# Loads of x issued from GpSimd instead of SyncE, and a ScalarE copy of the FFN split in two

## The chip, the cores and the metric

The kernel runs on the 8 cores of one Trainium2 chip. The cores run the same program on different data and exchange nothing. The metric is the device time of one execution, in microseconds (us), of the slowest core.

## The reference, cut to what matters

```python
# x: (4, 4096, 2048); D = 2048, 16 heads of 128, FFN width 8192
def attn(x):
    q, v = x @ Wq, x @ Wv                      # per head of 128 columns
    state[0] = v[0]; state[s] = lam * state[s-1] + v[s]      # lam = sigmoid(beta), per head
    y = layernorm(q * state) * ln_g + ln_b
    return (y * silu(x @ Wg)) @ Wo
def ffn(x):
    h = silu(x @ w_gate) * (x @ w_up)
    h = keep_the_2_largest_of_each_4(h)        # by absolute value
    return h @ w_down
x = x + layernorm(attn(layernorm(x)))
x = x + layernorm(ffn(layernorm(x)))
```

## The kernel before, in words

Each core has one half of one batch row: 2048 positions, as 16 tiles of 128. A core with a second half needs the state at its start, which it computes from the first half (`xprev`; zeros for the other cores). All weights come as float32 from HBM and are cast to bfloat16 in SBUF. Two SBUF slots, `wslotA` and `wslotB`, hold one 2048x2048 weight each. The stages, one after another:

- **Setup and weights.** `load_square_weight` brings Wq into `wslotA` and Wv into `wslotB`, each in 32 halves of 512 KB (`load_half`, line 606). SyncE issues the load into one of four staging quarters; ScalarE (line 617) and VectorE (line 613) take turns to cast. `lnab_bcast` (line 362) then brings ln_g and ln_b and spreads each over the partitions with matmuls (line 368) and a cast.
- **Carry prologue** (line 382): for each tile of `xprev`, load, layernorm, cast, and a matmul with decay weights that GpSimd (`iota`, line 394) and ScalarE make; then 256 small matmuls with Wv give `carry`.
- **Scan stage** (`attn_qv_scan`, line 443): for each tile `prep` loads x (line 446), takes statistics (line 310) and normalizes into `fp2`; TensorE transposes (line 336), ScalarE copies to SBUF (line 341), TensorE projects with Wq into PSUM `psB` and with Wv into `psA` (line 356), a matmul per head does the scan. ScalarE's copy of it (line 476) goes to VectorE, which multiplies by q (line 478), layernorms, and applies ln_g and ln_b (lines 496 and 499); GpSimd stores the result in `s_yaff` (line 502).
- **Gate stage** (`attn_gate`, line 505): Wg is loaded into `wslotA`. In iteration t TensorE transposes x(t) and projects it; `drain_ygT(t-1)` transposes the gated tile t-1 out of its `fp` buffer (line 336, VectorE evacuates at line 346) and GpSimd stores it in `s_ygT` (line 511); `prep(t+1)` loads x(t+1) into that same `fp` buffer (line 516) and normalizes it (line 519); ScalarE takes the silu (line 536), GpSimd loads `s_yaff` (line 538), VectorE multiplies (line 540).
- **Output stage** (`attn_out`, line 546): the first FFN weights (`load_q`) and Wo are loaded. In iteration t SyncE loads `s_ygT` (line 573) into `bp[t % 2]`, TensorE projects (line 356), `drain_xn3T(t-1)` transposes `fp2` (line 557), ScalarE copies it into `bp[(t-1) % 2]` (line 562) and GpSimd stores it in `s_xn3T` (line 566). VectorE layernorms the projection, x is loaded (line 586) and added (line 589), the sum goes to `s_x2` (line 592, shown as `s_x` in the trace) and is layernormed again (line 595). The load of ygT(t+1) takes the buffer that the store of xn3T(t-1) reads.
- **FFN** (`ffn`, line 638): 8 chunks of 1024 of the 8192 columns. For each chunk and tile: load `s_xn3T` (line 718), 32 gate matmuls (line 727), silu (line 732), 32 up matmuls (line 740), product (line 750), absolute value (line 755), nine VectorE instructions for the 2:4 mask (lines 765 to 788). Two tiles later (one in the last chunk) comes `drain`: 8 transposes of h into `psA` (line 675), a ScalarE copy back into h's own buffer as bfloat16 (line 680), 32 down matmuls into `psB` (line 689), VectorE's evacuation (line 697), and a store from GpSimd that adds into `s_acc` (lines 700 and 704). In the last chunk the final layernorm and addition follow.

**What sets the order.** `Prog.op` records operations; each engine runs its own in the order in which they are written, and a DMA belongs to the engine that issues it. An operation waits, by semaphores, for the last writer of each resource (`Res`) that it reads, and for the last writer and all readers since of each that it writes. The engine's own earlier instructions are waited for too, on all engines but TensorE. A resource has only one last writer:

```python
        for r in reads:
            if r.w is not None:
                toks.append(r.w)
...
        for w in writes:
            w.w = tok
            w.r = []
```

While an instruction waits, all that stands behind it on its engine waits, DMA issues included. SyncE issues all weight loads, the x loads, the `s_ygT`, `s_xn3T`, `s_acc` and `s_x2` loads and the output; GpSimd issues the stores to scratch tensors, the `s_yaff` loads and a few iotas.

## Time and profile before

| | |
|---|---|
| median of 2 runs | 6746.96 us (6743.37 to 6750.54) |
| the profiled execution | 6750.88 us |
| its span, slowest core (core 0) | 6749.3 us |
| spans of the 8 cores | 6694.7 to 6749.3 us |
| mean granted TensorE clock, core 0 | 0.856 |
| TensorE matmul busy | 4224.4 us (63%) |
| VectorE busy | 2060.5 us (31%) |
| ScalarE busy | 1003.0 us (15%) |
| GpSimd busy | 162.6 us (2%) |

The span runs from the first to the last instruction of a core. Busy shares are means over stages with different limits. All cores have nearly the same span, so core 0 stands for them. In the rows below the engines are PE (TensorE matmul), PEld (its weight loads), DVE (VectorE), ACT (ScalarE), POOL (GpSimd), and SPq for SyncE's issues of DMAs; L356 is line 356.

### The profile page before, as it was taken

The numbers are of one execution on the slowest core, as the hardware profiler recorded it, in microseconds if no ns is written. First come the engines' busy times: TensorE is split into PE (matmuls) and PEld (weight loads), VectorE is DVE, ScalarE is ACT, GpSimd is POOL, SyncE is SP. The second block draws the span as 40 slices with busy tenths as digits, with TensorE's granted clock in tenths as the row PEclk, the third lists the DMA queues.
The fourth block names the chain that finished last, engine by engine and source line by source line (L and its number), as shares of the span: only waits on it lengthen the run. The fifth ranks groups of instructions, "written<-read, shape, count | busy, mean of one in ns | idle before, by whom it ended". The sixth has DMA issues, their size and how long they took to land.

```text
span 6749.3 us, 51690 instructions; the slowest of 8 cores (6694.7 to 6749.3 us)
## 1 busy us (share of the span) xinstructions
PE 4224.4 (63%) x19374; PEld 1999.6 (30%) x19374; DVE 2060.5 (31%) x2796; ACT 1003.0 (15%) x1033; POOL 162.6 (2%) x232
## 2 busy tenths in 40 slices
PE   0236888456616668678678588498488487444443
PEld 0013444234303334334334234244244243111111
DVE  1533333212214433333333233233233233222222
ACT  2301111111111011111111111211211111111010
POOL 0000000000000000000000000000000000000000
PEclk9999888778758889889889799799799799777776
DMA  5300010222353331433533623623523534422223
GB/s 159 136 17 25 35 38 32 72 90 77 106 189 115 126 109 66 146 97 66 151 92 66 173 70 73 180 57 75 174 60 84 159 66 114 139 82 77 79 74 103
DMA packets 140830, 649.31 MB, mean 96 GB/s; under 512 B 15652, under 2 KB 15652, under 8 KB 107812
## 3 DMA queue, kind: packets, MB, share of 16 engines
q1 hardware_dynamic: 110630, 461.44, 20.9%
q0 software_dynamic: 29952, 184.56, 12.4%
q8 instruction: 156, 2.56, 0.2%
q14 instruction: 92, 0.75, 0.0%
HBM read 453.00 MB, written 192.94 MB: 96 GB/s over the span
## 4 chain that ended last, share of the span: by engine, by line
PE 59%; DMA 20%; DVE 10%; ACT 5%; issue 4%; SPq 1%; DVEq 0%; ACTq 0%; POOL 0%; POOLq 0%
PE psB L689 15%; PE psA L727 14%; PE psA L740 12%; PE psB L356 9%; PE psA L356 5%; DMA stg<-w_up 4%; DMA stg<-w_down 2%; PE psA L336 2%; DMA bp<-s_xn3T 2%; DMA s_acc<-wslotB 2%; ACT bp L755 2%; DMA stg<-Wo 1%; DVE stats L310 1%; DMA fp<-x 1%; DMA stg<-Wg 1%
## 5 line engine op out<-in xcount | busy, mean ns | idle before, releaser
L727 PE MATMUL psA<-wslotA,bp 128*128 128x512 bf16 x4096 | 954.4, 393 | 701.5 <-DMA bp<-s_xn3T 701.5
L740 PE MATMUL psA<-wslotA,bp 128*128 128x512 bf16 x4096 | 904.9, 379 | 0.0
L727 PEld LDWEIGHTS psA<-wslotA,bp 128*128 128x128 bf16 x4096 | 410.7, 101 | 1227.7 <-issue 778.0
L740 PEld LDWEIGHTS psA<-wslotA,bp 128*128 128x128 bf16 x4096 | 400.9, 98 | 483.2
L689 PE MATMUL psB<-wslotB,l_mat 128*128 128x512 bf16 x1440 | 344.6, 401 | 278.6 <-DVE bp L768 243.1
L356 PE MATMUL psB<-wslotA,bp 128*128 128x512 bf16 x2048 | 489.6, 404 | 44.2 <-ACT bp L341 44.2
L689 PE MATMUL psB<-wslotB,t_mat 128*128 128x512 bf16 x1472 | 357.9, 406 | 215.1 <-DVE bp L768 195.8
L356 PE MATMUL psA<-wslotB,bp 128*128 128x512 bf16 x1536 | 355.1, 394 | 212.5 <-DMA bp<-s_ygT 212.5
L697 DVE COPY wslotB<-psB 128x2048 f32<-128x2048 f32 x128 | 293.3, 2291 | 451.3 <-PE psB L689 451.3
L689 PE MATMUL psB<-wslotB,fp 128*128 128x512 bf16 x1184 | 280.4, 398 | 187.1 <-DVE bp L768 170.4
L732 ACT ACTIVATE fp<-psA 128x1024 f32<-128x1024 f32 x128 | 131.1, 1024 | 1510.8 <-PE psA L727 1510.7
L336 PE MATMUL psA<-ident,fp 128*128 128x128 f32 x768 | 145.0, 369 | 264.0 <-DVE fp L519 213.2
L356 PEld LDWEIGHTS psB<-wslotA,bp 128*128 128x128 bf16 x2048 | 208.2, 103 | 320.6 <-issue 111.4
L689 PEld LDWEIGHTS psB<-wslotB,l_mat 128*128 128x128 bf16 x1440 | 144.3, 102 | 467.5 <-issue 323.3
L613 DVE CAST wslotA<-stg 128x1024 bf16<-128x1024 f32 x160 | 111.0, 694 | 550.7 <-DMA stg<-w_up 322.8
L356 PEld LDWEIGHTS psA<-wslotB,bp 128*128 128x128 bf16 x1536 | 154.4, 101 | 408.7 <-issue 240.6
L689 PEld LDWEIGHTS psB<-wslotB,t_mat 128*128 128x128 bf16 x1472 | 148.8, 103 | 412.5 <-issue 268.6
L617 ACT CAST wslotA<-stg 128x1024 bf16<-128x1024 f32 x160 | 166.9, 1044 | 444.3 <-DMA stg<-w_gate 292.3
L750 DVE TENSOR_TENSOR t_mat<-psA,fp 128x1024 f32<-128x1024 f32 x46 | 56.3, 1224 | 568.0 <-PE psA L740 568.0
L310 DVE BATCH_NORM_STATS2 stats<-fp 128x6 f32<-128x512 f32 x256 | 158.0, 681 | 230.2 <-DMA fp<-s_acc 222.2
L750 DVE TENSOR_TENSOR l_mat<-psA,fp 128x1024 f32<-128x1024 f32 x45 | 55.1, 1225 | 545.3 <-PE psA L740 545.3
L689 PEld LDWEIGHTS psB<-wslotB,fp 128*128 128x128 bf16 x1184 | 117.7, 101 | 340.4 <-issue 220.4
(128 smaller groups left out, 3198.5 us busy)
## 6 DMA issues: line engine op xcount, KB each, us to landing
s_acc<-wslotB POOLq DMA_DIRECT2D x128, 1024.0 KB, 7.8
stg<-w_gate SPq DMA_DIRECT2D x128, 512.0 KB, 5.4
stg<-w_up SPq DMA_DIRECT2D x128, 512.0 KB, 5.9
stg<-w_down SPq DMA_DIRECT2D x128, 512.0 KB, 6.2
bp<-s_xn3T SPq DMA_DIRECT2D x128, 512.0 KB, 3.3
fp<-x SPq DMA_DIRECT2D x48, 1024.0 KB, 5.3
stg<-Wq SPq DMA_DIRECT2D x32, 512.0 KB, 4.6
stg<-Wv SPq DMA_DIRECT2D x32, 512.0 KB, 4.5
```

What stands on the lines that cost most here:

```text
L310: ins = v.bn_stats(st6[:, 6 * i:6 * i + 6], src_ap[:, 512 * i:512 * (i + 1)])
L336: ins = t.transpose(psA[:, half * 1024 + j * 128:half * 1024 + (j + 1) * 128], src_ap[:, kc * 128:(kc + 1) * 128], ident[:])
L356: ins = t.matmul(psum[:, n * 512:(n + 1) * 512], xT_ap[:, kc, :], w_sb[:, kc, n * 512:(n + 1) * 512], start=(kc == 0), stop=(kc == KC - 1))
L613: P.op("vector", lambda v, dst_ap=dst_ap, k=k: v.tensor_copy(dst_ap, wstg4[k]), reads=[r_wstg4[k]], writes=[dst_res, r_wstg4[k]])
L617: P.op("scalar", lambda s, dst_ap=dst_ap, k=k: s.copy(dst_ap, wstg4[k]), reads=[r_wstg4[k]], writes=[dst_res, r_wstg4[k]])
L689: ins = tt.matmul(psB[:, n * 512:(n + 1) * 512], hT[:, kc, :], fdc[:, kc, n * 512:(n + 1) * 512], start=(kc == 0), stop=(kc == ICW // 128 ...
L697: P.op("vector", lambda v, ev=ev: v.tensor_copy(ev[:], psB[:]), reads=[r_B[0], r_B[1]], writes=[r_stgF[dk], r_B[0], r_B[1]])
L727: ins = tt.matmul(psA[:, n * 512:(n + 1) * 512], xT[:, kc, :], fgc[:, kc, n * 512:(n + 1) * 512], start=(kc == 0), stop=(kc == KC - 1))
L732: P.op("scalar", lambda s, fx=fx: s.activation(fpool[fx][:, 0:ICW], psA[:, 0:ICW], AF.Silu), reads=[r_A[0]], writes=[r_fp[fx], r_A[0]])
L740: ins = tt.matmul(psA[:, 1024 + n * 512:1024 + (n + 1) * 512], xT[:, kc, :], fuc[:, kc, n * 512:(n + 1) * 512], start=(kc == 0), stop=(kc ...
L750: P.op("vector", lambda v, fx=fx, hsl=hsl: v.tensor_tensor(hsl[:, 0:ICW], psA[:, ICW:2 * ICW], fpool[fx][:, 0:ICW], ALU.mult), reads=[r_A[ ...
L755: P.op("scalar", lambda s, hsl=hsl: s.activation(habs[:, 0:ICW], hsl[:, 0:ICW], AF.Abs), reads=[rht], writes=[r_bp[2]])
```

## The change

First, six places at which SyncE issued a DMA now have GpSimd issue it: ln_g, ln_b, the tiles of `xprev`, and the tiles of x in the scan, the gate and the output stage. That is 2 + 16 + 48 loads. What they wait for and where they go stays. Second, in `drain`, the copy of 1024 columns is written as two copies of 512, each of which also writes a resource of its own, `rc[0]` or `rc[1]`, and the four groups of down matmuls read `rc[0]`, `rc[0]`, `rc[1]`, `rc[1]` besides `rh`.

```diff
     def lnab_bcast():
-        P.op("sync", lambda s: s.dma_start(out=fpool[0][0:1, :], in_=lng_d[:, :]), dma=True,
+        P.op("gpsimd", lambda g: g.dma_start(out=fpool[0][0:1, :], in_=lng_d[:, :]), dma=True,
              writes=[r_fp[0]])
...
-        P.op("sync", lambda s: s.dma_start(out=fpool[0][0:1, :], in_=lnb_d[:, :]), dma=True,
+        P.op("gpsimd", lambda g: g.dma_start(out=fpool[0][0:1, :], in_=lnb_d[:, :]), dma=True,
              reads=[r_fp[0]], writes=[r_fp[0]])
...
     def carry_prologue():
...
-            P.op("sync", lambda s, t=t, fx=fx: s.dma_start(
+            P.op("gpsimd", lambda g, t=t, fx=fx: g.dma_start(
                 out=fpool[fx][:], in_=xprev_d[t * 128:(t + 1) * 128, :]),
...
     def attn_qv_scan():
...
-            P.op("sync", lambda s, t=t, fx=fx: s.dma_start(
+            P.op("gpsimd", lambda g, t=t, fx=fx: g.dma_start(
                 out=fpool[fx][:], in_=x_d[t * 128:(t + 1) * 128, :]), dma=True,
                 writes=[r_fp[fx]])
...
```

The same edit stands in `prep` of `attn_gate` and, before the add, in `attn_out`. Then, in `drain`:

```diff
-            P.op("scalar", lambda s, hT_flat=hT_flat: s.copy(hT_flat[:, 0:ICW],
-                                                             psA[:, 0:ICW]),
-                 reads=[r_A[0]], writes=[rh, r_A[0]])
+            rc = [Res(), Res()]
+            for hh in range(2):
+                P.op("scalar", lambda s, hT_flat=hT_flat, hh=hh: s.copy(
+                    hT_flat[:, hh * 512:(hh + 1) * 512],
+                    psA[:, hh * 512:(hh + 1) * 512]),
+                     reads=[r_A[0]], writes=[rh, rc[hh], r_A[0]])
...
-                P.op("tensor", f, reads=[rh, r_fdc[q]], writes=[r_B[0], r_B[1]])
+                P.op("tensor", f, reads=[rh, rc[q // 2], r_fdc[q]],
+                     writes=[r_B[0], r_B[1]])
```

GpSimd's order in the gate stage, before (`bp3` holds the transposed gated tile, `bp2` the tile of `s_yaff`):

```order
L538 DMA bp2<-s_yaff 128x2048 [waits d_gpsimd5,d_gpsimd6]
L511 DMA s_ygT<-bp3 128x2048 [waits c_vector,d_gpsimd7]
L538 DMA bp2<-s_yaff 128x2048 [waits d_gpsimd8]
L511 DMA s_ygT<-bp3 128x2048 [waits c_vector,d_gpsimd9]
L538 DMA bp2<-s_yaff 128x2048 [waits d_gpsimd0]
```

And now (`fp0` and `fp1` are the buffers of x):

```order
L516 DMA fp0<-x 128x2048 [waits d_gpsimd5,d_gpsimd0]
L516 DMA fp1<-x 128x2048 [waits d_gpsimd7]
L538 DMA bp2<-s_yaff 128x2048 [waits d_gpsimd9,d_gpsimd2]
L511 DMA s_ygT<-bp3 128x2048 [waits c_vector]
L516 DMA fp0<-x 128x2048 [waits c_tensor,d_gpsimd4]
L538 DMA bp2<-s_yaff 128x2048
```

From the third load on, each load of x stands between a store of ygT, which waits for VectorE, and a load of yaff. The x loads had been alone on SyncE in this stage.

GpSimd's order in the output stage, before (`s_x2` is the stored sum, `s_xn3T` the transposed second layernorm):

```order
L566 DMA s_xn3T<-bp0 128x2048 [waits c_scalar,d_gpsimd9]
L592 DMA s_x2<-fp1 128x2048 [waits c_vector,d_gpsimd0]
L566 DMA s_xn3T<-bp1 128x2048 [waits c_scalar,d_gpsimd1]
L592 DMA s_x2<-fp0 128x2048 [waits c_vector,d_gpsimd2]
L566 DMA s_xn3T<-bp0 128x2048 [waits c_scalar,d_gpsimd3]
```

And now:

```order
L566 DMA s_xn3T<-bp0 128x2048 [waits c_scalar,d_gpsimd0]
L586 DMA fp1<-x 128x2048 [waits c_tensor,d_gpsimd1]
L592 DMA s_x2<-fp1 128x2048 [waits c_vector,d_gpsimd2]
L566 DMA s_xn3T<-bp1 128x2048 [waits c_scalar,d_gpsimd3]
L586 DMA fp0<-x 128x2048 [waits d_gpsimd4]
L592 DMA s_x2<-fp0 128x2048 [waits c_vector,d_gpsimd5]
```

The load of x(t) now follows the store of xn3T(t-1), and stands ahead of the store of x2(t).

ScalarE's order in the FFN, before (`t_mat`, `l3_mat` and `fp2` hold h in turn):

```order
L680 CAST t_mat<-psA 128x1024 [waits c_tensor]
L732 ACTIVATE fp1<-psA 128x1024 [waits c_tensor]
L755 ACTIVATE bp2<-t_mat 128x1024 [waits c_scalar,c_vector]
L680 CAST l3_mat<-psA 128x1024 [waits c_tensor]
L732 ACTIVATE fp0<-psA 128x1024 [waits c_tensor]
```

And now, where lines 682, 736 and 759 are what 680, 732 and 755 were:

```order
L682 CAST t_mat<-psA 128x512 [waits c_tensor]
L682 CAST t_mat<-psA 128x512 [waits c_scalar]
L736 ACTIVATE fp1<-psA 128x1024 [waits c_tensor]
L759 ACTIVATE bp2<-t_mat 128x1024 [waits c_vector]
L682 CAST l3_mat<-psA 128x512 [waits c_tensor]
L682 CAST l3_mat<-psA 128x512 [waits c_scalar]
```

The second copy of each pair waits for the first, ScalarE's own.

## Rows read from the trace of the kernel before

**Rows 1.** The page, part 4: the chain by line.
```profile
PE psB L689 15%; PE psA L727 14%; PE psA L740 12%; PE psB L356 9%; PE psA L356 5%; DMA stg<-w_up 4%; DMA stg<-w_down 2%; PE psA L336 2%; DMA bp<-s_xn3T 2%; DMA s_acc<-wslotB 2%; ACT bp L755 2%; DMA stg<-Wo 1%; DVE stats L310 1%; DMA fp<-x 1%; DMA stg<-Wg 1%
```

**Rows 2.** Timeline, gate stage, one tile: start us, us, engine, line [idle before].
```profile
1547.81 2.55 DVE L346 CAST bp<-psA 128x1024 bf16<-128x1024 f32 x2 [16.16 <-PE psA L336]
1548.56 27.73 SPq L516 DMA_DIRECT2D fp<-x  x2
1550.89 0.53 POOL L511 DMA_DIRECT2D s_ygT<-bp  x1 [26.16 <-DVE bp L346]
...
1553.84 1.35 DVE L519 TENSOR_SCALAR fp<-fp,ln1m,ln1r 128x2048 f32<-128x2048 f32 x1 [3.48 <-DMA fp<-x]
...
1560.05 13.97 PE L356 MATMUL psB<-wslotA,bp 128*128 128x512 bf16 x64 [1.25 <-ACT bp L341]
```

**Rows 3.** Timeline, output stage, one tile.
```profile
2112.53 0.53 POOL L566 DMA_DIRECT2D s_xn3T<-bp  x1 [21.16 <-ACT sd L315]
...
2115.41 2.29 DVE L589 TENSOR_TENSOR fp<-fp 128x2048 f32<-128x2048 f32 x1 [0.17 <-DVE fp L581]
2115.58 0.33 SPq L573 DMA_DIRECT2D bp<-s_ygT  x1
...
2119.03 15.27 PE L356 MATMUL psB<-wslotB,bp 128*128 128x512 bf16 x64 [8.54 <-DMA bp<-s_ygT]
```

**Rows 4.** Timelines of ACT and PE, FFN, one steady tile.
```profile
2647.91 0.99 ACT L680 CAST t_mat<-psA 128x1024 bf16<-128x1024 f32 x1
...
2649.15 7.07 PE L689 MATMUL psB<-wslotB,t_mat 128*128 128x512 bf16 x32 [2.76 <-DVE bp L768]
```

**Rows 5.** DMA issues, whole span: KB each, median us from issue to landing.
```profile
fp<-xprev SPq DMA_DIRECT2D x16, 1024.0 KB, 4.9
...
s_yaff<-bp POOLq DMA_DIRECT2D x16, 512.0 KB, 2.9
bp<-s_yaff POOLq DMA_DIRECT2D x16, 512.0 KB, 5.6
```

**Rows 6.** The chain in order of time, projections of the gate stage: start us, us.
```profile
1448.91 15.82 PE psB L356 x64
1478.18 13.97 PE psB L356 x64
...
1778.55 13.97 PE psB L356 x64
```

**Rows 7.** Timeline of DVE, end of the Wv load and start of lnab_bcast.
```profile
206.22 0.69 DVE L613 CAST wslotB<-stg 128x1024 bf16<-128x1024 f32 x1 [4.23 <-DMA stg<-Wv]
213.01 2.29 DVE L373 CAST stg<-psA 128x2048 bf16<-128x2048 f32 x1 [6.10 <-PE psA L368]
```

**Rows 8.** Timeline, carry prologue: GpSimd's second iota, VectorE's statistics of the third tile.
```profile
238.35 0.94 POOL L394 IOTA wlamT<- 16x128 f32 x1 [235.06 <-PE psB L401]
...
246.53 2.47 DVE L310 BATCH_NORM_STATS2 stats<-fp 128x6 f32<-128x512 f32 x4
```

**Rows 9.** Groups by line, scan stage: VectorE's product: busy us, mean ns | idle before us.
```profile
L478 DVE TENSOR_TENSOR stg<-psB,vst 128x2048 f32<-128x2048 f32 x16 | 36.7, 2292 | 443.3 <-ACT vst L476 443.3
```

**Rows 10.** Timeline, start of the gate stage.
```profile
1390.61 1.34 DVE L519 TENSOR_SCALAR fp<-fp,ln1m,ln1r 128x2048 f32<-128x2048 f32 x1 [1.80 <-DMA fp<-x]
```

**Rows 11.** ScalarE's copies out of PSUM: groups by line, and a timeline row.
```profile
L562 ACT CAST bp<-psB 128x1024 bf16<-128x1024 f32 x16 | 16.2, 1012 | 117.4 <-PE psB L557 116.4
...
L423 ACT CAST xbarT<-psB 128x256 bf16<-128x256 f32 x1 | 0.4, 372 | 2.1 <-PE psB L419 2.1
...
2055.65 2.17 ACT L562 CAST bp<-psB 128x1024 bf16<-128x1024 f32 x2 [15.70 <-PE psB L557]
```

**Rows 12.** The chain in order of time, second chunk: first and last slow drain.
```profile
2977.58 8.75 PE psB L689 x32
...
3254.04 8.75 PE psB L689 x32
```

**Rows 13.** Timeline of POOL, end of the gate stage.
```profile
1841.73 0.99 POOL L511 DMA_DIRECT2D s_ygT<-bp  x1 [13.41 <-DVE wslotA L613]
```

More of the change, by code:

```diff
@@ L515, in prep @@
             fx = t % 2
-            P.op("sync", lambda s, t=t, fx=fx: s.dma_start(
+            P.op("gpsimd", lambda g, t=t, fx=fx: g.dma_start(
                 out=fpool[fx][:], in_=x_d[t * 128:(t + 1) * 128, :]), dma=True,
@@ L585, in attn_out @@
                  writes=[r_fp[2], rpso[0], rpso[1]])
-            P.op("sync", lambda s, t=t, fx=fx: s.dma_start(
+            P.op("gpsimd", lambda g, t=t, fx=fx: g.dma_start(
                 out=fpool[fx][:], in_=x_d[t * 128:(t + 1) * 128, :]), dma=True,
```

## The prediction

> **What bounds the kernel now.** I read the page's chain first [rows 1]: most of it is TensorE, spread over all stages, so what an edit is worth must be read inside its stage. Then I took one tile of each stage in the timeline and asked what the first matmul after each gap waited for.
>
> *Gate stage* [rows 2]: after the projection TensorE transposes tile t-1, which frees the buffer, SyncE issues the load of x(t+1) at 1548.56, VectorE normalizes it at 1553.84 as soon as it lands, and after two transposes and copies the next projection starts at 1560.05. The load of x is on the chain. VectorE's two evacuations end at 1547.81 + 2.55 = 1550.36, GpSimd issues the store of ygT at 1550.89 and the load of yaff right behind it, at 1550.89 + 0.53 = 1551.42; those two delay nobody.
>
> *Output stage* [rows 3]: projection t+1 waits for ygT(t+1), loaded by SyncE at 2115.58 as soon as the store of xn3T(t-1), issued by GpSimd at 2112.53, has landed. The x(t) needed by the add at 2115.41 had long been there.
>
> *FFN, steady* [rows 4]: TensorE works without a gap but for one, 2.76 us a tile, between the transposes of h and the down matmuls. ScalarE's copy (2647.91 + 0.99 = 2648.90) ends 0.25 us before the matmuls start (2649.15). The profile names DVE L768 as releaser, an instruction that happens to end nearby; by the code's own waits it is the copy.
>
> **The change part by part.**
>
> **1. x loads on GpSimd, gate stage.** GpSimd issues in program order: store ygT(t-1), load x(t+1), load yaff(t). So x(t+1) now waits for VectorE's evacuations. It takes yaff's slot, which is 1551.42 - 1548.56 = 2.86 us later, and stands behind 512 KB of ygT. 1 MB alone lands in 4.9 us (xprev), 512 KB alone in 2.9 as a store (s_yaff) and in 3.45 as a load (2119.03 - 2115.58) [rows 3, 5], so a further 512 KB costs 1.5 to 2.0; I take 1.8. The pair, 1.5 MB, lands at 1550.89 + 4.9 + 1.8 = 1557.6 instead of 1553.84: +3.8 us. If both move side by side for free, 1551.42 + 4.9 = 1556.3 and +2.5 us; if x is also slowed as bp<-s_yaff is, 5.6 against 2.9, by 2.7, it is more than the pair needs, and I cap it at +4.5. The load is delayed in tiles 2 to 15 (x(0), x(1) are issued before the first store): 14 x 3.8 = +53 us (35 to 63). The last of them no longer competes with w_gate loads: -1.
>
> **2. The clock in that stage.** A projection takes 15.82 us when it starts at the low level (1.2 GHz) and 13.97 when it runs at 2.4 GHz [rows 6]; the 12 from 1478.18 to 1778.55 are all fast. The gap ahead of them grows by more than half. I let half of the 12 start low: 6 x 1.9 = +11 us (0 to 22).
>
> **3. Output stage.** Order on GpSimd: store xn3T(t-1), load x(t), store x2(t). x(t) is now issued at 2112.53 + 0.53 = 2113.06 and moves its 1 MB while xn3T lands and while ygT(t+1), on SyncE's queue, is loaded. Before, the next x stood behind ygT on the same queue and cost it little (3.45 us). If the two queues share, ygT loses the time in which x has the other half: x, alone, is over at about 2113.06 + 4.9 = 2118.0, ygT moves data in the last 1.5 to 2 us of its 3.45, so about 1.2 us are lost; the most contended 512 KB load shows 5.6 against 3.5, 2.1 us [rows 3, 5]. 14 x 1.2 = +17 (0 to 30). The add gets x(t) some 3 to 4 us late (lands 2118 to 2119.5 against 2115.41), with no one waiting: the transposes of that tile come only after the next projection, at 2119.03 + 15.27 = 2134.3 and later. After the last tile nothing covers it: +4 (2 to 6) before the FFN starts. The first ygT no longer shares with two x loads: -1.
> The Trainium skill ("DMA: Bandwidth & Descriptors", section "SWDGE vs HWDGE vs iDMA") says that software and hardware descriptors sit in different internal queues of a DMA engine, which serves them in turn. By that rule ygT shares with x, as I take it; were it first come first served, ygT would wait for all of x's rest and the term would be nearer its upper end. No row of before shows this pair.
>
> **4. Start.** ln_g is needed only by its matmuls, and its load was queued behind the last Wv load. On GpSimd it comes at the very start, the matmuls run during the weight load, and VectorE's cast follows its last weight cast at 206.22 + 0.69 = 206.91 instead of 213.01 [rows 7]: -6 us (the ln_b half keeps its length).
>
> **5. Carry prologue and scan stage.** xprev(t+2) now also waits for GpSimd's iota, over at 238.35 + 0.94 = 239.29, and lands by 239.29 + 0.53 + 4.9 = 244.7; it is used at 246.53 [rows 8]. Nothing, 1.8 us of cover; if 2 us were added per load, a few us in all. In the scan stage x(t+2) waits for the store of yaff(t); VectorE's statistics come some 7 us later, but it idles 443.3 / 16 = 27.7 us a tile after them [rows 9]: nothing.
>
> **6. Entry of the gate stage.** x(0) is no longer behind the Wg loads: -3 (-5 to 0), the 1.80 us that VectorE waited for it [rows 10] and a little bandwidth.
>
> **7. The split copy.** The second half's copy writes rh too, so rh's last writer is the second copy, and the very first down matmul reads rh: it waits for both. rc only matters if rh did not stand beside it. So nothing starts early. The price: 256 columns take 0.372 us, 1024 take 0.99, so 512 take about 0.372 + 256 x (0.99 - 0.372) / 768 = 0.58. The second copy waits for the first one's semaphore; two such copies of the output stage take 2.17 in a row where 2 x 1.012 are work, a gap of 0.15 [rows 4, 11]. 0.58 + 0.15 + 0.58 = 1.31 against 0.99: +0.32 us a drain (0.25 to 0.40). On the path are the 13 steady drains of 7 chunks and 16 of the last, 107 x 0.32 = 34; at the chunk borders are 21 more, where other waits may cover between none and all of 0.32; I take 0.1, +2. Together +36 (27 to 50).
>
> **8. The clock in the FFN.** Of the 13 steady drains of a chunk, 5 run at the low level part of the time, 8.75 us instead of 7.07 (2977.58 the first, 3254.04 the last) [rows 4, 12]. The clock had fallen in the gap; it grows from 2.76 to 3.08. I take 6.5 of 13: 1.5 x 7 x 1.68 = +18 (0, to 8 x 7 x 1.68 = 94 if all do).
>
> **Sum**: 53 - 1 + 11 + 17 + 4 - 1 - 6 - 3 + 36 + 18 = **+128 us** on the profiled 6750.9, which is 3.9 above the median shown, 6747. From the median: **6875 us**, 1.9% slower.
>
> **The rivals.**
> A, *the queues hardly hinder each other*: x costs only its later issue (14 x 2.5 = 35), ygT loses 5, the clock nothing. 35 - 1 + 5 + 3 - 1 - 6 - 3 + 34 = +66, 6813 us. For it: ygT's load hardly suffered from the x load behind it. Against it: yaff's load takes 5.6 us in company.
> B, *the clock decides*: every steady drain falls to the low level. 94 instead of 18: +204, 6951 us. For it: the gap is already one at which 5 in 13 fall. Against: most 2.76 us gaps leave it up, and 0.3 us is little. It passes 2% from about one more slow drain per chunk than I take.
> C, *the split works*: the first matmuls start on the first half, 0.99 - 0.58 = 0.41 us earlier. 107 x 0.41 = -44, the shorter gap spares all slow drains, 35 x 1.68 = -59, and the loads still cost 53 - 1 + 11 + 17 + 4 - 1 - 6 - 3 = +74: -29, 6718 us, not slower. Against: the shared rh.
> D, *GpSimd's issue is stretched by VectorE*: one store issue beside VectorE's casts took 0.99 us instead of 0.53 [rows 2, 13]. 28 x 0.46 = 13 more: 6888 us. Against: in the gate stage VectorE is idle when x is issued. The Trainium skill ("SBUF — State Buffer", the "DVE blocks DMA" box) has this as a rule; by this row the trace agrees in kind.
>
> **How the numbers follow.** Mine 0.60 (0.34 of it within 2%, 0.26 above), A 0.17, B 0.13, D 0.06, C 0.04 (half of it faster by over 2%). 2%, 135 us, about what a measurement of this kernel can tell from no change, ends at 6882. So faster 0.02, same 0.53, slower 0.45. Range 6810 to 6935: it holds A and D and leaves out B and C.
>
> **What would show it.** In the gate stage: x issued by POOL after ygT's store, the tile at 31 us instead of (1778.55 - 1478.18) / 11 = 27.3, and the chain's share of fp<-x larger. Projections of 15.8 among them show part 2. Output stage: the ygT load above 3.5 us. FFN: two copies of about 0.58 us, the gap at 3.1, and the count of 8.7 us drains. I am wrong if the gap falls below 2.76 (C), if the gate tile grows by under 2.5 us, or if the steady FFN tile grows by over 1 us (B).

## The result, and the profile after

The changed kernel is slower: the ratio of its time to that of the kernel before is **1.0295, 95% interval 1.024 to 1.0349**. That is 6946 us on 6747; I had said 6875, with 6935 as the upper end. The direction was right and the size too small. The ratio is taken over six executions of either kernel: 6743 to 6755 us before; five of 6926 to 6940 us and one of 7019 us now. The five alone would give 6929 us, just inside my range, so that the range was missed is less certain than that the sum was too small. The profiled execution took 6936.59 us, with a span of 6934.9 us on core 4, the slowest; the kernel before had 6750.88 and 6749.3 us on core 0. In some executions one half of the chip ran at a lower clock than the other; such executions are left out, but for the one of 7019 us, where the difference was small, and where the experiments name cores 4 to 7, only that half was undisturbed.

The page of the changed kernel: the chain by line, and two rows of the DMA issues (KB each, median us from issue to landing).

```profile
PE psB L692 14%; PE psA L731 13%; PE psA L744 12%; PE psB L356 9%; PE psA L356 5%; DMA stg<-w_up 5%; DMA stg<-w_down 2%; DMA bp<-s_xn3T 2%; PE psA L336 2%; DMA s_acc<-wslotB 2%; DMA fp<-x 1%; DMA stg<-Wg 1%; DMA bp<-s_ygT 1%; DVE stats L310 1%; DMA stg<-Wv 1%
...
bp<-s_xn3T SPq DMA_DIRECT2D x128, 512.0 KB, 3.3
fp<-x POOLq DMA_DIRECT2D x48, 1024.0 KB, 6.8
```

Beside [rows 1] the chain has nearly the same members. bp<-s_ygT and stg<-Wv are new in the list, at 1% each, ScalarE's line 755 (2%) and stg<-Wo (1%) have dropped out of it, and the shares of three lines moved by a point. A change of 2.95% spread over four stages does not stand out in it. So the span is cut at TensorE's own landmarks, start times in the timeline: the first and last projection of a stage, the first gate matmuls of a chunk. The columns before and after are from the slowest core of each trace, and so is the difference; the column beside it takes the means over all 8 cores of the same two traces.

| stretch of the span, us | before | after | difference | 8 cores | predicted |
|---|---|---|---|---|---|
| start to end of the scan's last projection | 1273.4 | 1267.4 | -6.0 | -6.5 | -6 |
| entry: to the start of the first gate projection | 123.6 | 131.7 | +8.1 | +3.3 | -3 |
| gate stage: first to last projection, start to start | 410.0 | 494.0 | +84.0 | +89.6 | +63 |
| from the end of the last to the first output projection | 170.2 | 165.0 | -5.2 | +0.9 | -1 |
| output stage: first to last projection, start to start | 393.1 | 425.9 | +32.8 | +28.9 | +17 |
| from the end of the last to the first gate matmul of the FFN | 48.2 | 51.3 | +3.1 | +4.3 | +4 |
| FFN, 7 chunks | 3376.5 | 3436.7 | +60.2 | +55.3 | +54 with the last |
| FFN, last chunk, to its last down matmul | 893.3 | 902.0 | +8.7 | +11.0 | |
| **sum** | | | **+185.7** | **+186.8** | **+128** |

The sum is the difference of the spans, 6934.9 - 6749.3 = 185.6. (The last projections of the two stages and the tail behind the last down matmul are in no line; they take 61 us in both.) The FFN came nearest (69 against 54); the gate and output stages and the entry are too small by 21, 16 and 11. One pair of cores carries a few us of chance a line: by the means over 8 cores they are too small by 27, 12 and 6.

**Gate stage.** The timeline of one tile.

```profile
1605.29 1.91 PE L336 MATMUL psA<-ident,fp 128*128 128x128 f32 x16
...
1606.57 2.55 DVE L346 CAST bp<-psA 128x1024 bf16<-128x1024 f32 x2 [19.85 <-PE psA L336]
...
1609.73 0.54 POOL L511 DMA_DIRECT2D s_ygT<-bp  x1 [32.30 <-DVE bp L346]
1610.30 0.53 POOL L516 DMA_DIRECT2D fp<-x  x1
1610.82 0.53 POOL L538 DMA_DIRECT2D bp<-s_yaff  x1
1617.39 1.35 DVE L519 TENSOR_SCALAR fp<-fp,ln1m,ln1r 128x2048 f32<-128x2048 f32 x1 [8.27 <-DMA fp<-x]
```

The order is the one forecast: VectorE's evacuations, the store of ygT, x, yaff. From VectorE's start at the evacuations, 1606.57, to the normalization, 1617.39, it is 10.82 us; in [rows 2] it was 1553.84 - 1547.81 = 6.03. That is +4.8 in this tile, where I took 3.8: the issue of x moved as forecast (3.73 us after VectorE's start; before 0.75, so 2.98 later), but the load then needs 1617.39 - 1610.30 = 7.1 us instead of 5.3. As a mean over tiles 2 to 15 it is +4.5 (core 0 before, core 4 now) to +4.7 (core 5 in both), at my cap of 4.5 or just above it. From 1487.53 to 1859.78, eleven tiles, a tile takes 33.8 us, against 27.3 before. The rest is in the projections. TensorE's timeline, three in a row:

```profile
1695.64 12.16 PE L356 MATMUL psB<-wslotA,bp 128*128 128x512 bf16 x54 [0.22 <-issue]
1724.94 13.97 PE L356 MATMUL psB<-wslotA,bp 128*128 128x512 bf16 x62 [1.25 <-ACT bp L341]
1757.37 15.62 PE L356 MATMUL psB<-wslotA,bp 128*128 128x512 bf16 x63 [1.25 <-ACT bp L341]
```

(The first is the second part of a projection that began at 1691.85 and took 15.95 in all; the row is split where a record is missing.) Of the twelve that took 13.97 us in [rows 6], one still does; the others take 15.5 to 16.0. The sum over the third to the fifteenth projection rose from 183.5 to 202.1 us, +18.6. 14 x 4.5 to 4.8 and 18.6 make 82 to 86, of the 84 in the table.

**Entry.** The timeline ahead of the gate stage:

```profile
1285.95 33.34 SPq L610 DMA_DIRECT2D stg<-Wg  x9
1287.31 1.06 POOL L516 DMA_DIRECT2D fp<-x  x2 [0.35 <-issue]
...
1303.19 0.69 DVE L613 CAST wslotA<-stg 128x1024 bf16<-128x1024 f32 x1 [17.32 <-DMA stg<-Wg]
```

The two first x loads are now issued 1.4 us after the first Wg load, and move 2 MB ahead of the Wg loads that follow. SyncE's nine Wg issues, each paced by a staging buffer that comes free, are spread over 33.3 us; in the trace of before the same nine took 23.9. VectorE waits 17.32 us for the first of its halves, against 9.28. I had counted only that x came earlier. The cost is smaller than this pair of cores shows: the entry's mean over 8 cores is 126.1 us before, 129.3 here and 129.7 to 129.8 in the three experiments in which GpSimd loads this x at once (b, c and e below).

**Output stage.** The timeline of one tile:

```profile
2199.54 0.53 POOL L566 DMA_DIRECT2D s_xn3T<-bp  x1 [17.74 <-ACT sd L315]
2200.07 0.53 POOL L586 DMA_DIRECT2D fp<-x  x1
...
2203.08 30.14 SPq L573 DMA_DIRECT2D bp<-s_ygT  x2
...
2207.86 2.29 DVE L589 TENSOR_TENSOR fp<-fp 128x2048 f32<-128x2048 f32 x1 [5.61 <-DMA fp<-x]
2209.56 16.31 PE L356 MATMUL psB<-wslotB,bp 128*128 128x512 bf16 x62 [12.05 <-DMA bp<-s_ygT]
```

ygT is issued at 2203.08 and lets the projection go at 2209.56: 6.48 us, against 3.45 in [rows 3] (as means of the stage's tiles 6.2 and 3.6). The store of xn3T takes 2203.08 - 2199.54 = 3.54 until the buffer is free (3.05 before). TensorE's idle time ahead of a projection rose from 8.65 to 11.55 us, as means over the stage's 15 gaps, +2.9 x 15 = 43. The 16 projections gave 259.5 - 251.7 = 7.8 back, as more of their work fell into fast clock: 43 - 8 = 35, of the 33 in the table. VectorE waits 5.61 us for x(t) and nobody waits for VectorE there, as forecast.

How ygT loses its time is not as forecast. The DMA queues' packets between 2203.4 and 2206.3 us, which begins just after ygT's issue (queue, packets, MB, share of the 16 DMA engines):

```profile
q0 software_dynamic: 99, 0.81, 76.6%
```

and between 2206.3 and 2209.6:

```profile
q1 hardware_dynamic: 144, 0.52, 38.8%
q0 software_dynamic: 34, 0.15, 10.9%
```

q0 is GpSimd's queue and carries x, q1 is SyncE's and carries ygT. For some 3 us ygT does not move at all, while x has the engines; all of ygT's packets come when x is nearly over. Over the stage, ygT's first packet comes 0.96 us after its issue before the change, and 2.7 to 4.1 us after it now. So ygT does not share the engines with x: it waits behind the whole of it.

**FFN.** TensorE's timeline, three steady drains in a row:

```profile
3131.24 7.07 PE L692 MATMUL psB<-wslotB,fp 128*128 128x512 bf16 x32 [3.01 <-ACT fp L682]
3156.00 8.75 PE L692 MATMUL psB<-wslotB,t_mat 128*128 128x512 bf16 x31 [3.01 <-ACT t_mat L682]
3182.45 7.07 PE L692 MATMUL psB<-wslotB,l_mat 128*128 128x512 bf16 x31 [3.01 <-ACT l_mat L682]
```

and ScalarE's:

```profile
3154.50 1.24 ACT L682 CAST t_mat<-psA 128x512 bf16<-128x512 f32 x2
```

The two copies take 1.24 us together (0.99 was one, [rows 4]); the gap is 3.01 us, 0.25 more than the 2.76 before, and this time the profile names the copy itself as the releaser. Nothing starts early. Here drains at 8.75 and at 7.07 us alternate. Counting the down matmuls of the 7 chunks that take over 7.6 us, there are 54 of 112, and were 40. From the first to the last steady drain of each chunk TensorE took 2287.9 us before and 2333 after, +45, which is 91 x 0.25 = 23 and 14 more slow drains x 1.68 = 24 (46 in all).

### The profile page after: what moved, and what is told of

Read it like the earlier page. It is cut to its first block, busy times and chain, and to the rows that moved or that the text cites. A ratio compares the mean times of both kernels' runs of the same rounds, so it can differ in the third digit from the quotient of the medians.

```text
span 6934.9 us, 51439 instructions; the slowest of 8 cores (6895.5 to 6934.9 us)
## 1 busy us (share of the span) xinstructions
PE 4227.8 (61%) x19010; PEld 2008.5 (29%) x19374; DVE 2060.0 (30%) x2796; ACT 1023.0 (15%) x1161; POOL 198.3 (3%) x298
## 4 chain that ended last, share of the span: by engine, by line
PE 58%; DMA 21%; DVE 9%; issue 6%; ACT 5%; SPq 1%; DVEq 0%; ACTq 0%; POOL 0%; POOLq 0%
PE psB L692 14%; PE psA L731 13%; PE psA L744 12%; PE psB L356 9%; PE psA L356 5%; DMA stg<-w_up 5%; DMA stg<-w_down 2%; DMA bp<-s_xn3T 2%; PE psA L336 2%; DMA s_acc<-wslotB 2%; DMA fp<-x 1%; DMA stg<-Wg 1%; DMA bp<-s_ygT 1%; DVE stats L310 1%; DMA stg<-Wv 1%
## 5 line engine op out<-in xcount | busy, mean ns | idle before, releaser
L701 DVE COPY wslotB<-psB 128x2048 f32<-128x2048 f32 x128 | 293.3, 2291 | 507.6 <-PE psB L692 507.6
L336 PEld LDWEIGHTS psA<-ident,fp 128*128 128x128 f32 x768 | 133.6, 198 | 348.1 <-issue 345.0
```

Source lines behind the costliest of these rows:

```text
L336: ins = t.transpose(psA[:, half * 1024 + j * 128:half * 1024 + (j + 1) * 128], src_ap[:, kc * 128:(kc + 1) * 128], ident[:])
L701: P.op("vector", lambda v, ev=ev: v.tensor_copy(ev[:], psB[:]), reads=[r_B[0], r_B[1]], writes=[r_stgF[dk], r_B[0], r_B[1]])
```

## The experiments

What I held after the result: (1) the split copy costs 50 to 70 us and the moved loads the rest, and the two hardly meet; (2) in the gate stage it is the order on GpSimd's queue that delays x, plus the clock; (3) in the output stage it is that x moves at the moment at which ygT does, not who issues it; (4) the number of slow drains follows the gap. Each has its rival in the texts below. Most of the experiments rest on one execution each, so they are read by stage, over its cores, and the difference of the spans is the weaker sign.

### The two halves of the change

`a_split_only` is the kernel before with only the change in `drain`; `b_moves_only` is the changed kernel with that part put back.

```diff
+            rc = [Res(), Res()]
+            for hh in range(2):
+                P.op("scalar", lambda s, hT_flat=hT_flat, hh=hh: s.copy(
...
+                     reads=[r_A[0]], writes=[rh, rc[hh], r_A[0]])
```

> The kernel before with the split copy alone. Theory 1 (the split costs its own gap, and the longer gap makes TensorE's clock fall more often): gap before the down matmuls 3.0 us instead of 2.76, about one steady drain in two at 8.7 us instead of 5 in 13, the FFN 60 to 70 us longer, ratio 1.009 to 1.011. Rival (the FFN grew in the changed kernel because the moved loads shifted it against the clock or the DMAs): only the gap's 0.25 x 128 = 32 us, ratio about 1.005, drains slow as often as before.

Measured: span 6791.8 us, executions of 6793 and 6797 us, beside 6740 and 6750 of the kernel before on the same chip, +43 to +57; but two more of the kernel before took 6779 and 6809 us there, so the times alone would not settle it. The stages ahead of the FFN are as before (gate 408.6, output 390.6 us on core 5). The steady part of the FFN is 2329 to 2336 us over the cores, as in the changed kernel (2331 to 2338), and the slow drains are 51 to 56, one in two, as Theory 1 had it. The whole FFN is 41 us longer by the means over 8 cores, less than the 60 to 70 of Theory 1 and more than the rival's 32.

> The changed kernel with the copy in one piece again: only the loads are moved. Theory 1 (the two edits add up): everything up to the FFN as in the changed kernel, the FFN as before, 6749 + 116 = about 6865 us span, ratio 1.016 to 1.018. Rival (the parts interact, the moved loads also lengthen the FFN): above 1.020.

Measured: span 6858.7 us, executions of 6860 and 6862; ratio 1.0135, interval 1.0039 to 1.0232, slower than the kernel before but too wide to say whether by 2%. Gate 491 to 497 us, output 413 to 422, the FFN's 7 chunks 3361 to 3371 with 40 to 42 slow drains. So the FFN does not feel the moved loads alone, and the stages before it do not feel the split. By the spans the halves give 42.5 + 109.4 = 152 of 186. The rest is in the FFN: by the means over 8 cores it grew by 41 us with the split, by -4 with the moved loads, and by 66 with both. Its steady part is the same in a and in the changed kernel, so these 29 us arise at the chunk borders and in the last chunk, where the halves do meet; how, no run here shows.

### The moved loads, stage by stage

`c_gate_only` and `d_out_only` move the x load of one stage alone. The edit of c, in `attn_gate`; that of d is the same in `attn_out`:

```diff
         def prep(t):
             fx = t % 2
-            P.op("sync", lambda s, t=t, fx=fx: s.dma_start(
+            P.op("gpsimd", lambda g, t=t, fx=fx: g.dma_start(
```

> The kernel before with only the gate stage's loads of x on GpSimd. Theory 1 (the loss lies in that stage's own queue): first to last projection of the stage 494 us instead of 410, its start 8 us later than the end of the scan stage was before, the output stage as before; span about 6749 + 84 + 8 - 5 = 6836. Rival (the stage suffers from what the other moved loads leave behind, a shifted clock or semaphores reused in another order): under +40 in that stage.

Measured: span 6838.7 us, +89. The gate stage takes 493 to 504 us, the entry 128 to 133; the output stage 391 to 400 and the FFN's 7 chunks 3362 to 3377 us. The gate load alone makes that stage's loss. The entry, too: it had been 124 to 129 on the cores of the kernel before, and is 3.7 us longer in the mean.

> The kernel before with only the output stage's loads of x on GpSimd. Theory 1 (x shares the DMA engines with the load of ygT, which the projection waits for): first to last projection of that stage 426 us instead of 393, ygT landing in 6.5 us instead of 3.45, span about 6749 + 33 + 3 = 6785. Rival (the stage is longer only because the gate stage before it changed): 393 us, no change in the time.

Measured: span 6762.7 us, +13, less than expected: the output stage takes 410 to 418 us, 21 more than before in the mean over 8 cores where the changed kernel has 29 more, and the FFN, which this edit does not touch, came out 13 us shorter on the slowest core. The timeline on core 5:

```profile
2113.68 0.53 POOL L566 DMA_DIRECT2D s_xn3T<-bp  x1 [17.43 <-ACT sd L315]
...
2117.07 29.83 SPq L573 DMA_DIRECT2D bp<-s_ygT  x2
...
2123.12 16.61 PE L356 MATMUL psB<-wslotB,bp 128*128 128x512 bf16 x64 [11.47 <-DMA bp<-s_ygT]
```

The load of ygT takes 2123.12 - 2117.07 = 6.05 us, and TensorE waits 11.47: the pattern of the changed kernel, from this one edit.

### Issuer, queue position, or company?

`g_out_x_early` leaves x(t) on GpSimd but records it at the top of the iteration, ahead of `drain_xn3T`, so it is issued at the start of the projection, well before ygT's load.

```diff
+            P.op("gpsimd", lambda g, t=t, fx=fx: g.dma_start(
+                out=fpool[fx][:], in_=x_d[t * 128:(t + 1) * 128, :]), dma=True,
+                writes=[r_fp[fx]])
             if pend is not None:
                 drain_xn3T(pend)
```

> The output stage's loads of x on GpSimd, but recorded ahead of the store of xn3T(t-1), so that they run early, during the projection; all else as before. Theory 1 (ygT lands late because x moves at the same moment): ygT lands in about 3.5 us again, first to last projection 388 to 396 us, span as before. Rival (GpSimd's queue is slower, or more traffic there delays the stores of xn3T): 410 us or more.

Measured, cores 4 to 7: output stage 387 to 393 us, as before the change; spans 6719.8 to 6738.0. Core 5:

```profile
2107.93 27.30 SPq L573 DMA_DIRECT2D bp<-s_ygT  x2
...
2111.34 16.78 PE L356 MATMUL psB<-wslotB,bp 128*128 128x512 bf16 x64 [8.88 <-DMA bp<-s_ygT]
```

3.41 us for ygT, the 3.45 of [rows 3]. GpSimd as issuer costs the path nothing; x just ahead of ygT costs some 2 to 3 us a tile. The Trainium skill ("DMA: Bandwidth & Descriptors", section "SWDGE vs HWDGE vs iDMA") has the engines serve software and hardware queues in turn. If so, a turn here is a whole transfer: no packet of ygT moves between 2203.4 and 2206.3 us, and the load that alone needs 3.45 us takes 6.48 and 6.05 because it waits for x. The section "Issuing engines are not separate DMA queues" of the same page of the Trainium skill says that transfers run on the same engines and interleave whoever starts them. That they meet on the same engines, g and d bear out; that they interleave, the rows of the changed kernel do not show, as there ygT follows x.

`e_gate_x_first` has x on GpSimd ahead of the store of ygT; `f_gate_sync_late` leaves it on SyncE but makes it wait for the evacuations. The edit of e:

```diff
+
+        def store_ygT(t):
             P.op("gpsimd", lambda g, t=t: g.dma_start(out=s_ygT[t], in_=bpool[3][:]),
                  dma=True, reads=[r_bp[3]], writes=[r_sygT[t]])
...
-            P.op("sync", lambda s, t=t, fx=fx: s.dma_start(
+            P.op("gpsimd", lambda g, t=t, fx=fx: g.dma_start(
...
             if t + 1 < NT:
                 prep(t + 1)
+            if pend is not None:
+                store_ygT(pend)
```

and of f:

```diff
                 out=fpool[fx][:], in_=x_d[t * 128:(t + 1) * 128, :]), dma=True,
-                writes=[r_fp[fx]])
+                reads=[r_bp[3]], writes=[r_fp[fx]])
```

> The gate stage's loads of x on GpSimd as in the changed kernel, but each recorded ahead of the store of ygT, so that it waits for TensorE's transposes alone. All other loads as before. Theory 1 (the place in the queue costs, not the engine): x is issued about 2 us after the transposes begin and lands some 5.3 us later, the tile is back at 27.3 to 28 us, first to last projection 405 to 415 us, projections mostly 13.97 us. Rival (a load issued by GpSimd is itself slower): landing near 7 us, tiles of 30 us or more, 450 us.

> The kernel before, all loads on SyncE, but the gate stage's load of x also waits for VectorE's second evacuation, as it does behind the store of ygT. Theory 1 (the wait costs what it lasts, about 2.3 us a tile, the common queue the rest, and the longer gap makes the projections start at the low clock): x issued 2.4 us later, landing in 5.3 to 6 us, tile about 30 us plus 1.7 where the projection starts low, stage 445 to 475 us. Rival (all of the 6.6 us a tile come from the delay and the clock): 495 us.

Measured: e has a gate stage of 443 to 446 us, f one of 452 to 454 (cores 4 to 7). The timeline of e, core 0:

```profile
1559.94 1.91 PE L336 MATMUL psA<-ident,fp 128*128 128x128 f32 x16
...
1562.54 0.54 POOL L518 DMA_DIRECT2D fp<-x  x1 [27.28 <-DVE bp L346]
...
1568.19 1.34 DVE L521 TENSOR_SCALAR fp<-fp,ln1m,ln1r 128x2048 f32<-128x2048 f32 x1 [4.42 <-DMA fp<-x]
```

and of f, core 5:

```profile
1547.29 13.97 PE L356 MATMUL psB<-wslotA,bp 128*128 128x512 bf16 x64 [1.25 <-ACT bp L341]
...
1561.10 1.91 PE L336 MATMUL psA<-ident,fp 128*128 128x128 f32 x16
...
1565.00 0.33 SPq L516 DMA_DIRECT2D fp<-x  x1
...
1571.23 1.34 DVE L519 TENSOR_SCALAR fp<-fp,ln1m,ln1r 128x2048 f32<-128x2048 f32 x1 [6.30 <-DMA fp<-x]
```

From the start of the transposes to the normalization: 7.3 us before (the transposes ahead of [rows 2] start at 1546.53), 8.25 in e, 10.13 in f, 12.1 in the changed kernel. (The means over tiles 2 to 15 are 7.2 to 7.4, 8.4 to 8.6, 10.3 and 11.9 to 12.0.) So moving the issue alone to GpSimd costs 0.95 us in this tile; waiting for the evacuations, on SyncE, costs 2.8, of which 1.9 is the later issue and 0.9 a slower landing; standing behind the store on GpSimd's queue brings the 4.8. So the delay of x is mostly a matter of the queue's order. Whether yaff, issued right behind x, slows it too was not tested. But by that e should have been at 410.0 + 14 x 0.95 = 423, and f at 449. f is at 453; e is at 444, above the 405 to 415 of my theory and near the rival's 450, though its x is hardly late: the load was used 5.65 us after its issue, not 7. What lies between is the clock. TensorE's timeline of e, core 5:

```profile
1606.30 16.02 PE L356 MATMUL psB<-wslotA,bp 128*128 128x512 bf16 x64 [1.25 <-ACT bp L341]
1636.74 16.16 PE L356 MATMUL psB<-wslotA,bp 128*128 128x512 bf16 x64 [1.25 <-ACT bp L341]
```

and the gate stage as a window, in e on core 5 and in f on core 5 (window, its length, busy us of PE, PEld, DVE, ACT, POOL, granted clock, DMA share, GB/s):

```profile
1404.00:1848.00 444.00, 311.73 (x1424) 171.07 (x1423) 86.90 (x58) 59.78 (x46) 22.44 (x42) 0.80 0.19 67
```

```profile
1400.58:1854.00 453.42, 294.67 (x1424) 167.69 (x1424) 86.08 (x58) 59.46 (x46) 14.90 (x28) 0.82 0.21 69
```

In e, with the shorter gap, TensorE works 311.7 us for the same matmuls; in f, with the longer one, 294.7, as most of its projections take 13.97. A tile lasts some 30.4 us in either. Smaller windows show where the low clock lies, in e at the start of a projection and in f in the projection that begins at 1577.61:

```profile
1575.60:1579.80 4.20, 4.19 (x11) 1.44 (x11) 0.00 (x0) 0.00 (x0) 0.00 (x0) 0.51 0.02 4
```

```profile
1577.60:1591.60 14.00, 13.99 (x66) 6.50 (x67) 0.00 (x0) 0.00 (x0) 0.00 (x0) 1.00 0.00 1
```

In e the clock is low (1.2 GHz) from 1566.1 to 1579.8, 4.2 us into the projection; in f from 1566.3 to 1576.5, and high again before the projection starts. So in this stage the low clock does not simply grow with the gap ahead of a projection (about 14.4 us in e, 16.4 in f): in e the low stretch is longer, and reaches into the projection. I had expected neither, and why the two differ I can't say from these traces.

### The split and the gap

`i_split_four` makes four dependent copies of 256 columns; `h_split_free` makes two that depend on nothing of each other, and lets each group of down matmuls wait only for its own half. Both edits are shown against the changed kernel's `drain`, i first:

```diff
-            for hh in range(2):
+            for hh in range(4):
...
-                    hT_flat[:, hh * 512:(hh + 1) * 512],
-                    psA[:, hh * 512:(hh + 1) * 512]),
-                     reads=[r_A[0]], writes=[rh, rc[hh], r_A[0]])
+                    hT_flat[:, hh * 256:(hh + 1) * 256],
+                    psA[:, hh * 256:(hh + 1) * 256]),
+                     reads=[r_A[0]], writes=[rh, rc[hh // 2], r_A[0]])
```

```diff
-                P.op("scalar", lambda s, hT_flat=hT_flat, hh=hh: s.copy(
+                tk = P.op("scalar", lambda s, hT_flat=hT_flat, hh=hh: s.copy(
...
-                     reads=[r_A[0]], writes=[rh, rc[hh], r_A[0]])
+                     reads=[r_A[0]], writes=[rc[hh]])
+                rh.r.append(tk)
...
-                P.op("tensor", f, reads=[rh, rc[q // 2], r_fdc[q]],
+                tk = P.op("tensor", f, reads=[rc[q // 2], r_fdc[q]],
+                          writes=[r_B[0], r_B[1]])
+                rh.r.append(tk)
```

> The kernel before with the copy in four parts of 256 columns, each waiting for the one before, all waited for by the first down matmul. So far a gap of 2.35 us left almost no steady drain slow, 2.76 us 5 in 13, 3.0 us 1 in 2. Theory 1 (the longer the gap, the more often the clock falls): copies 4 x 0.37 + 3 x 0.07 = 1.7 us, gap about 3.4 us, 2 in 3 steady drains slow or more, FFN 59 (gap) + 40 to 60 (clock) us longer than before. Rival (the place in time decides, as it did in the gate stage, where 0.95 us of delay made most projections slow and 2.8 us few): gap 3.4 us and no more slow drains than 1 in 2, FFN 60 to 85 us longer.

> The kernel before with the copy split in two so that it works: the first two groups of down matmuls wait for the first half alone, and the second copy does not wait for the first. Theory 1 (the gap ahead of the down matmuls decides how often the clock falls): gap about 2.35 us, 107 x 0.4 = 43 us less, and slow drains rarer than 5 in 13, so 60 to 100 us less in the FFN. Rival (the drains fall by their place in time, not by the gap's length): 43 us less and 5 in 13 slow as before.

Measured, i: span 6925.3 us, the FFN's 7 chunks 3513 to 3525 us, 150 more than before in the mean, and the last chunk 29 more, where Theory 1 had 99 to 119 in all. TensorE and ScalarE on core 5:

```profile
3155.32 8.75 PE L692 MATMUL psB<-wslotB,l_mat 128*128 128x512 bf16 x32 [3.50 <-DVE bp L775]
3182.27 7.07 PE L692 MATMUL psB<-wslotB,fp 128*128 128x512 bf16 x32 [3.50 <-DVE bp L775]
```

```profile
3126.39 1.74 ACT L682 CAST t_mat<-psA 128x256 bf16<-128x256 f32 x4
```

Measured, h: span 6656.4 us, an execution of 6658 beside 6737 of the kernel before; 7 chunks 3279 to 3295 us, 83 less than before in the mean.

```profile
3041.34 7.07 PE L693 MATMUL psB<-wslotB,l_mat 128*128 128x512 bf16 x32 [2.34 <-DVE bp L771]
...
3065.43 7.07 PE L693 MATMUL psB<-wslotB,fp 128*128 128x512 bf16 x32 [2.34 <-DVE bp L771]
```

```profile
3040.52 1.05 ACT L682 CAST l_mat<-psA 128x512 bf16<-128x512 f32 x2
```

In h, the matmuls start (3041.34) before the second copy ends (3040.52 + 1.05 = 3041.57). The four kernels give a series, with the least and the most over the 8 cores:

| | gap, us | slow drains of 112 | steady part, us |
|---|---|---|---|
| split, halves free (h) | 2.34 | 17 to 20 | 2210 to 2215 |
| before | 2.76 | 39 to 42 | 2286 to 2291 |
| split as changed, and a | 3.01 | 51 to 56 | 2329 to 2338 |
| four dependent copies (i) | 3.50 | 78 to 84 | 2419 to 2428 |

Each step, taken from 19, 40 and 81 slow drains and 2212, 2288 and 2425 us, is explained by 91 x (difference of the gap) + (difference of slow drains) x 1.68: h 38 + 35 = 73 of 76; i 67 + 70 = 137 of 137. In the FFN, with 22 us of matmuls between gaps, the share of slow drains grows steadily with the gap (even at 2.34 us, 10 to 13 of the 91 steady ones are slow, not "almost no" drain, as the text on i has it); at no point on the way did all of them fall. Beyond the steady part, i lost 42 us more at the chunk borders and in the last chunk than this accounts for.

### Freeing the buffer instead

If the x load of the gate stage waits for a buffer, and ygT's in the output stage for another, then other buffers should give what no change of issuer can. `l_gate_ahead` loads x(t), from t = 2, into the staging buffers that are idle once Wg is in, and records `prep(t+1)` ahead of the projection; `m_out_buffers` lets `drain_xn3T` use `bpool[2]` and `bpool[3]`; `k_combined` is l, m and h together, with ln_g and ln_b on GpSimd.

```diff
+            if t < 2:
+                xb, rx = fpool[fx], [r_fp[fx]]
+            else:
+                xb, rx = stg[fx], [r_stg[fx], r_wstg4[2 * fx], r_wstg4[2 * fx + 1]]
...
+            if t + 1 < NT:
+                prep(t + 1)
             proj_mms(xT, r_bp[bx], wslotA, r_wA, psB, [r_B[0], r_B[1]])
```

```diff
-                    bpool[bx][:, half * 1024:(half + 1) * 1024],
+                    bpool[2 + bx][:, half * 1024:(half + 1) * 1024],
```

> The kernel before with the gate stage's x(2) to x(15) loaded by SyncE into the two staging buffers, idle there, and normalized during the projection ahead. Theory 1 (the wait for x is the gap): the gap between projections shrinks from 13.4 us to about 6, projections stay at 13.97 us, first to last projection near 410 - 14 x 7.4 = 306 us, span 100 us less. Rival (another wait ends close behind it, VectorE's evacuations or the copies): under 50 us less.

> The kernel before with the output stage's xn3T copied into two other buffers, so that the load of ygT(t+1) does not wait for the store of xn3T(t-1). Theory 1 (that load, with the store ahead of it, is the gap of 8.5 us): gap about 2.6 us, first to last projection near 393 - 14 x 6 = 309 us, span 80 us less, if VectorE's 15.5 us of work per tile keep up. Rival (VectorE bounds the tile at once): 350 us.

> The two stage changes of the kernels sent beside it, the copy split so that the first matmuls wait for the first half alone, and ln_g and ln_b loaded by GpSimd; all x loads stay on SyncE. Theory 1 (each works in its own stage): 100 + 80 + 85 + 6 us less, near 6480 us, ratio 0.96. Rival (the stages give back: a higher clock demand or the loads of the next stage's weights become late): above 6560 us.

Measured, l (cores 4 to 7): gate stage 302 to 305 us, spans 6621.4 to 6651.4, about 100 us less than before. Core 5, one tile:

```profile
1530.37 13.97 PE L356 MATMUL psB<-wslotA,bp 128*128 128x512 bf16 x64 [1.25 <-ACT bp L341]
...
1535.97 1.34 DVE L523 TENSOR_SCALAR fp<-stg,ln1m,ln1r 128x2048 f32<-128x2048 f32 x1
...
1544.18 1.91 PE L336 MATMUL psA<-ident,fp 128*128 128x128 f32 x16
```

The normalization of the next tile (1535.97) now lies beside the projection, with no wait for x, and a tile takes 20.1 us.

Measured, m: span 6618.7 us, output stage 262 to 265 us instead of 388 to 396. Core 5:

```profile
2069.81 0.33 SPq L574 DMA_DIRECT2D bp<-s_ygT  x1
2070.65 2.17 ACT L562 CAST bp<-psB 128x1024 bf16<-128x1024 f32 x2 [6.48 <-PE psB L557]
...
2073.07 12.25 PE L356 MATMUL psB<-wslotB,bp 128*128 128x512 bf16 x56 [1.70 <-ACT bp L562]
2073.41 0.53 POOL L566 DMA_DIRECT2D s_xn3T<-bp  x1 [11.44 <-ACT sd L315]
```

The projection starts before the store of xn3T is even issued; ygT had been loaded a tile ahead. The projections run at 13.97 us again, 259.5 - 226.5 = 33 us less in sum: with the wait gone the clock comes back too (granted 0.99 over the stage, against 0.83 before, on core 5). Most of what the stage gained beyond the 84 us that I expected is that.

Measured, k: spans 6401.5 to 6437.4 us; executions of 6439 and 6416 us, beside 6748 of the kernel before on the same chip. That is 309 to 332 us or 4.6 to 4.9% less, from two executions against one, so without an interval.

```profile
core 6: 6437.4 us, clock 0.876
```

The three gains, 93 and 131 by the spans of h and m and some 100 for l, add up to 324, against 6749.3 - 6437.4 = 312 here; by the means over the cores they are 90, 126 and 95, and with the 6 us of ln_g 316 against 314. So they add up. The clock of the slowest core went from 0.856 to 0.876. k beats both kernels.

## Why the prediction was right or wrong

The step that failed is the overlap in part 3: I let ygT share the DMA engines with x, and it waited for all of x. Beside it stand a term that was mis-sized (1), one whose reason does not hold (2) and one of the wrong sign (6). By its own steps:

- **1, x behind the store of ygT: right in kind, mis-sized.** I had bounded it at 2.5 to 4.5 us a tile and took 3.8; it measured 4.8 in the tile shown and 4.5 to 4.7 in the mean, at my cap or above it. The part that I underrated is the landing: 7.1 us behind 512 KB of ygT, where I gave it 1557.6 - 1551.42 = 6.2. 14 x 1.0 = 14 us.
- **2, the clock in the gate stage: inside its bounds, but the reason does not hold.** I let half of the twelve fast projections start low (+11, at most +22). Eleven of twelve did: +18.6. Behind it stood the thought that a longer gap makes more of them slow; e and f show that this is not the rule here, since the longer gap had the faster projections. So that the number came near is partly luck.
- **3, the output stage: the step that failed, mis-sized by two.** That x delays ygT was right, and d and g confirm it. But 1.2 us a tile supposed that the two share the engines, with x soon over. Measured: +2.9 of idle time a tile, 43 us in all, because ygT's packets come only when x's are nearly over (first packet 2.7 to 4.1 us after the issue, 0.96 before). That is the case that I had named beside the sum as first come, first served, with the term nearer its upper end of 30; the projections gave 8 back, and the stage came out at +33 (+29 in the mean over the cores). Tail: +3 against +4.
- **4, start, and 5, prologue and scan:** -6 and nothing, and -6.0 is what came.
- **6, entry: wrong sign.** -3 against +8 in this pair of cores, and against +3.3 to +3.7 in the means over 8 cores, here and in b, c and e. I wrote of VectorE's wait for x and "a little bandwidth" and did not ask what x(0) and x(1), free to start, would move beside: the first Wg loads, for which both casting engines wait. This is the one place where the question "what will the earlier transfer collide with" was left out.
- **7, the split: right.** No early start, confirmed by a and, by the counter-case, h. +0.25 us a drain, at the lower end of 0.25 to 0.40: two copies take 1.24 and not 1.31 us.
- **8, the clock in the FFN:** 1.5 more slow drains a chunk taken, (54 - 40) / 7 = 2.0 measured.

Of the rivals, A (queues hardly hinder) fell by the gate and output stages. B (all drains slow) fell: half of them are; its time, 6951, is close to the measured one for another reason, so a total alone would have confirmed the wrong case. C (the split works) fell, though h shows that the idea was good and only the shared `rh` stood in its way; freed, it gives 93 us. D (GpSimd's issue stretched) fell: POOL is busy 198.3 us with 298 instructions against 162.6 with 232, so 35.7 us for 66 more, 0.54 each, which is the unstretched 0.53. The Trainium skill's "DVE blocks DMA" box ("SBUF — State Buffer") would have such issues stretched; this case does not show it on the moved loads.

The total missed by 58 us, and four terms that were all too low make most of it: parts 1, 2, 3 and 6 with 14 + 7 + 16 + 11 = 48. All four concern DMA in company, or the clock in the gap that it leaves. The trace of before had a sign of it that I did not read: in the gate stage the stores of ygT, issued by GpSimd 2.3 us behind x on SyncE's queue, took 4.1 us where the stores of yaff took 2.9 alone. The FFN adds 69 - 54 = 15, mostly at the chunk borders and there only with both halves of the change, and the small terms take 5 off. By the means over 8 cores the gate stage was short by 27, the output stage by 12, the entry by 6 and the FFN by 12.

## What to carry to other kernels

A load that is moved to another engine's queue takes on what that queue waits for, and whatever is issued just behind it on another queue may have to wait for it whole: look for its new neighbours in time before counting what its old queue gains. A split of a producer helps only if each consumer waits for its own part; with one shared resource it adds an instruction to the path. Where a load waits for a buffer, give it another buffer; here that was worth 100 and 130 us in two stages where changing the issuer cost 84 and 33.

## What the runs showed that I had not expected

- The share of slow drains is graded: about 19, 40, 54 and 78 to 84 of 112 at gaps of 2.34, 2.76, 3.01 and 3.50 us. From the first to the last that is (81 - 19) / 11.6, some 5 more per 0.1 us of gap, or 5 x 1.68 / 112 = 0.08 us a drain: nearly as much as the gap itself costs.
- In the gate stage a longer gap (f) went with a faster projection than a shorter one (e), at the same tile length of 30.4 us. How long the low stretch lasts and where it ends decided it; what sets that stays open.
- A 512 KB load took 3.41 to 3.45 us alone and 6.05 to 6.48 when a 1 MB load had been issued on another queue 3 us ahead of it. The two did not share the engines: the smaller one's packets came after nearly all of the larger one's.
- Taking the wait out of the output stage raised the clock as well: its 16 projections fell from 259.5 to 226.5 us in sum, 33 of the 129 us that the stage gained in m.
